# A three-stage transformer kernel whose per-sequence walk is written out in full instead of running as loops over two sequences

## The chip, the cores and the metric

The kernel runs on one core of one Trainium2 chip. The metric is the device time of one execution in microseconds (us), lower is better. Three runs of the kernel before gave 2319.28, 2320.09 and 2324.1 us, so the median is 2320.09 us.

## What is computed

There are 16 sequences of 512 tokens with 128 features, all float32. Two sandwiched blocks are applied to them:

```python
x = L0_attn_x                                     # (16, 512, 128)
x = x + layernorm(attn(layernorm(x)))             # 16 heads of 8, 4 key groups, causal, rotary
x = x + layernorm(ffn(layernorm(x)))
# ffn: two layers, each
#   qkv = shift_token(x) @ wqkv[l]                # 8 heads of 64
#   q, k = l2norm(q) * qs, l2norm(k) * ks; rotary with position scales
#   x = x + local_attention(q, k, v) @ wo[l]      # windows of 64, each looks one window back
#   h = layernorm(shift_token(x)) @ w1[l] + b1[l]
#   x = x + (a * gelu(g)) @ w2[l] + b2[l]
```

## The kernel before

The program has three stages, each in a block of its own with an instruction stream for every engine. `causal_attention` is the first main stage: it makes the first sandwich for the 16 sequences and leaves normalised, transposed activations in the SBUF buffer `u`. `local_layers` is the second main stage: two layers, each over the 16 sequences, `u` in and `u` out. `last_norm` is a short closing stage over four groups of four sequences.

In both main stages the order of the work is written out by hand as a list (`ORDER1`, `ORDER`). Each entry is a task with a part number. A *step* b runs the whole list once: part 0 tasks work on sequence b+1, part 1 tasks on sequence b, part 2 tasks on sequence b-1. So three sequences are in flight, and one sequence is finished in each step. In the first stage the last task of a step's part 2 is `copy_u` (line 532, ACT, two instructions); in the second it is `result` (line 1215, DVE, two instructions). The interval between two of these is the length of a step.

`walk` (lines 88 to 117) is called by each engine for itself and issues that engine's tasks. It writes step -1 (once) and steps 0, 1 and 2 straight out, then opens a hardware loop `eng.Fori(3, B - 2, 2)` whose body holds two steps, b and b+1; it runs six times, for steps 3 to 14, and so jumps back five times. Step 15 is again straight code. The second main stage does this once for each of its two layers. That makes 18 passes through a body and 15 jumps back in the whole program, on each engine: PE, ACT, DVE, POOL and SP (which issues the DMAs). The engines loop independently; there is no barrier at the end of a pass, only the semaphores of the tasks.

The order between engines is kept by semaphores that are only ever counted up. `Plan.linear` gives the value to wait for: where the sequence number is a Python integer it returns an integer; inside the loop the number is a register, and it returns `b * each + constant`, which the engine's sequencer works out with register instructions in front of the wait (seen in the profile at lines 140, 146, 151 and 286). The buffer slot (`slot`) is a Python integer in either case, since the body holds an even and an odd step. Line 113 is the loop itself: its register set-up, its compare and its branch.

Line 1272 holds the transposes of q and k on PE, line 1319 the products of probabilities and values.

Of the kernel before, what the change touches and what calls it, by code (L numbers as in the profile page):

```python
# [15 lines left out]
B, T, D = 16, 512, 128  # L16
# [71 lines left out]
def walk(eng, plan, tasks):  # L88

    def place(l, b, part):
        if not isinstance(b, int):
            return l, b + (1 - part)
        n = l * B + b + 1 - part
        return divmod(n, B) if 0 <= n < plan.depth * B else None

    def step(l, b, slot):
        for part, name, arg, *_ in plan.order:
            at = place(l, b, part)  # L100
            if at is None:
                continue
            for before, before_arg in plan.ahead(at[1], name, arg):
                if before in tasks:
                    tasks[before](*at, before_arg, slot ^ (part != 1))
            if name in tasks:
                tasks[name](*at, arg, slot ^ (part != 1))

    step(0, -1, 1)
    for l in range(plan.depth):  # L110
        for b in range(3):
            step(l, b, b % 2)
        with eng.Fori(3, B - 2, 2) as b:
            step(l, b, 1)
            step(l, b + 1, 0)
        step(l, B - 1, 1)
    step(plan.depth, 0, 0)


# [169 lines left out]
def causal_attention(nc, sem, ident, ident_bf, x1_v, u, x_v, Wq, bq, Wk, bk, Wv, bv, Wo, bo, cos1, sin1):  # L289
    with ExitStack() as ctx:  # L290
# [76 lines left out]
        def _(sp):  # L367
# [26 lines left out]
            for dst, src in loads:  # L394
                sp.dma_start(dst, src).then_inc(consts_loaded, 16)
            walk(sp, PLAN1, dict(load=load, load_again=load_again, store=store))
            for slot in range(2):
                sp.wait_ge(x1_stored[slot], 8 * B)

        @block.gpsimd  # L400
        def _(pool):
# [78 lines left out]
            def residual(l, b, arg, slot):  # L480
# [3 lines left out]
                pool.tensor_tensor(x1[:, slot], x_again[:, slot], z[:], ALU.add).then_inc(x1_made, 1)  # L484

            walk(pool, PLAN1, dict(apply=apply, rope_cos=rope_cos, rope_sin=rope_sin, rope_add=rope_add, copy_v=copy_v, low=low,
                                   select=select, residual=residual))

        @block.scalar
        def _(act):  # L490
# [38 lines left out]
            def copy_u(l, b, arg, slot):  # L529
                x, read = flow.to_read(act, "u_turn", 0, l, b)  # L530
                for r, first in ((slice(0, DH), 0), (slice(DH, P), 1)):
                    last = act.copy(u[r, bass.ds(b, 1), first:first + T].rearrange("p a t -> p (a t)"), x[r, :])
                last.then_inc(read, 1)

            walk(act, PLAN1, dict(seed=seed, copy_x=copy_x, copy_k=copy_k, copy_q=copy_q, copy_max=copy_max, exp=exp,
                                  copy_o=copy_o, copy_attn=copy_attn, copy_u=copy_u))

# [981 lines left out]
```

## Time and profile before

| | kernel before |
|---|---|
| median of three runs | 2320.09 us |
| the profiled execution, whole time | 2322.1 us |
| its span, first to last instruction | 2320.0 us |
| PE (matmuls) busy | 2048.2 us, 88% |
| DVE busy | 1819.0 us, 78% |
| ACT busy | 1634.9 us, 70% |
| POOL busy | 1381.1 us, 60% |
| mean granted TensorE clock | 0.948 |

PE is the tensor engine's matmuls and PEld its weight loads; they share one instruction stream. DVE, ACT and POOL are the vector, scalar and general engines. A *q* behind an engine's name (PEldq) means its sequencer: register instructions, branches and waits, which are not counted as busy time. [...] "issue" as the cause of an idle stretch means that the profile shows nothing that the engine waited for. Times in the rows are counted from the span's start.

### The profile page before, as it was taken

The page shows a single profiled execution, that of the slowest core. Times are in us where ns is not written, and L with a number is a line of the kernel's source. Part 1 is how long each engine was busy: PE and PEld are TensorE (multiplying, and loading weights), DVE is VectorE, ACT ScalarE, POOL GpSimd, SP SyncE. Part 2 cuts the span into 40 slices and gives each one's busy share as a digit, 9 for nine tenths or more (in the row PEclk, how much of TensorE's full clock was granted, in tenths as well). Part 3 has the DMA queues.
Part 4 walks back from the last instruction along what each step waited for, and adds up shares of the span by engine and source line. Part 5 has one row for each costly group of instructions (what it writes and reads, how often), then busy time and mean ns, then how long its engine had stood idle before and what let it go on. Part 6 is the DMA issues. An engine that isn't in the chain of part 4 may idle for free. (4 is left out here: it accounts for less than half of the span.)

```text
span 2320.0 us, 57840 instructions
## 1 busy us (share of the span) xinstructions
PE 2048.2 (88%) x20476; PEld 1354.5 (58%) x20476; DVE 1819.0 (78%) x3455; ACT 1634.9 (70%) x3312; POOL 1381.1 (60%) x2090
## 2 busy tenths in 40 slices
PE   2999999999999369999999999899999999999971
PEld 1555555555554256666666666566666666666641
DVE  2788788788786376988888888896898898798746
ACT  1676676676676266887787787786877787777745
POOL 3688787787786564655655655554564564564403
PEclk8999999999999579999999999999999999999985
DMA  1010000000000011010010010111011001001013
GB/s 35 2 28 16 16 24 19 16 18 26 15 15 20 28 48 32 18 34 18 18 34 18 18 34 18 28 34 31 18 25 28 19 20 32 18 18 34 18 37 110
DMA packets 50539, 60.13 MB, mean 26 GB/s; under 512 B 8144, under 2 KB 43392, under 8 KB 48256
## 3 DMA queue, kind: packets, MB, share of 16 engines
q1 hardware_dynamic: 50304, 56.58, 9.8%
q8 instruction: 199, 3.26, 0.6%
q14 instruction: 36, 0.29, 0.0%
HBM read 17.90 MB, written 8.39 MB: 11 GB/s over the span
## 5 line engine op out<-in xcount | busy, mean ns | idle before, releaser
L985 POOL TENSOR_TENSOR b_part_b<-b_raw,b_tabs 128x256 f32<-128x256 f32 x512 | 431.7, 874 | 345.6 <-ACT b_raw L1044 310.9
L994 POOL TENSOR_TENSOR b_qk<-b_qk,b_part_b 128x1024 f32<-128x1024 f32 x128 | 332.5, 2598 | 270.2 <-DVE b_qk L1144 263.0
L1144 DVE TENSOR_TENSOR b_qk<-b_raw,b_tabs 128x512 f32<-128x512 f32 x256 | 301.8, 1218 | 0.1
L1245 PE MATMUL b_work<-b_w_high,b_h_high 128*128 128x512 f32 x384 | 191.2, 498 | 31.0 <-DVE b_h_low L1134 19.2
L476 POOL TENSOR_SCALAR_AFFINE_SELECT a_probs<-a_probs 128x256 f32<-128x256 f32 x512 | 207.5, 418 | 0.0
L425 POOL TENSOR_TENSOR a_idle<-a_idle 128x1 f32<-128x1 f32 x432 | 84.7, 196 | 197.7 <-ACT a_probs L519 131.2
L1272 PE MATMUL b_work<-ident,b_qk 128*128 128x128 f32 x1024 | 162.1, 290 | 42.0 <-issue 32.0
L690 PE MATMUL a_work<-a_probs,a_v 128*32 128x512 f32 (+3 forms) x2048 | 182.2, 452 | 7.1 <-POOL a_probs L476 7.0
L1319 PEld LDWEIGHTS b_work<-b_v_even,b_pT 128*64 128x64 f32 x2048 | 140.8, 141 | 79.4 <-issue 76.7
L1272 PEld LDWEIGHTS b_work<-ident,b_qk 128*128 128x128 f32 x1024 | 127.1, 149 | 87.7 <-issue 65.1
L1065 ACT ACTIVATE b_probs<-b_sb,b_neg_max 128x128 f32<-128x128 f32 x512 | 147.9, 384 | 41.4 <-DVE b_neg_max L1166 41.0
L587 DVE TENSOR_REDUCE a_qpack<-a_pc 128x2 f32<-128x768 f32 (+1 forms) x128 | 139.4, 1089 | 43.9 <-PE a_pc L658 41.9
L1319 PE MATMUL b_work<-b_v_even,b_pT 128*64 128x66 f32 x2048 | 171.9, 231 | 2.0 <-ACT b_pT L1071 0.8
L1071 ACT COPY b_pT<-b_work 128x512 f32<-128x512 f32 x256 | 154.2, 602 | 25.4 <-PE b_work L1309 25.2
L1319 PE MATMUL b_work<-b_v,b_pT 128*64 128x66 f32 x2048 | 172.1, 232 | 0.0
L1033 ACT ACTIVATE b_sq<-b_work 128x1024 f32<-128x1024 f32 x128 | 131.5, 1027 | 56.6 <-PE b_work L1247 53.8
L1138 DVE TENSOR_REDUCE b_ss<-b_sq 128x16 f32<-128x1024 f32 x128 | 155.2, 1212 | 20.7 <-ACT b_sq L1033 17.5
L1160 DVE TENSOR_TENSOR b_qk<-b_qk,b_rs 128x1024 f32<-128x1024 f32 x128 | 163.9, 1282 | 4.9 <-POOL b_qk L994 2.2
L587 DVE TENSOR_REDUCE a_qpack<-a_pa 128x2 f32<-128x1024 f32 (+3 forms) x128 | 148.1, 1157 | 18.8 <-PE a_pa L658 14.4
L1309 PE MATMUL b_work<-ident,b_probs 128*128 128x128 f32 x1024 | 158.0, 278 | 4.6 <-ACT b_kT L1052 2.8
L1173 DVE RECIPROCAL b_rden<-b_work 128x4 f32<-128x4 f32 x256 | 45.5, 178 | 144.7 <-PE b_work L1319 140.0
L1309 PEld LDWEIGHTS b_work<-ident,b_probs 128*128 128x128 f32 x1024 | 126.0, 143 | 53.9 <-issue 36.3
(211 smaller groups left out, 5642.7 us busy)
## 6 DMA issues: line engine op xcount, KB each, us to landing
b_v_even<-b_v SPq DMA_DIRECT2D x32, 528.0 KB, 4.4
b_v_even<-b_v SPq DMA_DIRECT2D x32, 396.0 KB, 5.8
a_x_in<-in_L_attn_x SPq DMA_DIRECT2D x16, 256.0 KB, 3.5
a_x_again<-in_L_attn_x SPq DMA_DIRECT2D x16, 256.0 KB, 3.5
x_scratch<-a_x SPq DMA_DIRECT2D x16, 256.0 KB, 2.4
out<-c_y SPq DMA_DIRECT2D x4, 1024.0 KB, 5.4
b_w_raw<-in_L_ffn_wqkv SPq DMA_DIRECT2D x2, 768.0 KB, 4.3
b_tabs<-tab SPq DMA_DIRECT2D x2, 512.0 KB, 4.0
```

What stands on the lines that cost most here:

```text
L476: last = pool.affine_select(out=a, in_=a, compare_op=ALU.is_ge, fill=0.0, base=0, pattern=[[0, 2], [1, P]], channel_multiplier=-1)
L587: dve.tensor_reduce(qpack[:, slot, i, js[0]:js[-1] + 1, two, NEG_MAX].rearrange("p j g -> p g j"), x[:, :, 0:len(js) * w].rearrange("p g ( ...
L690: last = pe.matmul(bank_of[which][groups(g), s * P:T], v[:, slot, s, g, :], probs_of(j, fill + g % 2)[:, g // 2, col:col + T - s * P], sta ...
L985: last = pool.tensor_tensor(part_b[:, x, :].rearrange("p (h d) -> p h d", d=DH)[:, :, lo:lo + DH // 2], raw[:, i % 2, x, :].rearrange("p ( ...
L994: pool.tensor_tensor(qk[:, i], qk[:, i], part_b[:], ALU.add).then_inc(c_made, 1)
L1138: dve.tensor_reduce(ss[:, i * 16:(i + 1) * 16], sq[:].rearrange("p x (h d) -> p (x h) d", d=DH), AX, ALU.add).then_inc(ss_made, 1)
L1144: last = dve.tensor_tensor(qk[:, i, x, :].rearrange("p (h d) -> p h d", d=DH), raw[:, i % 2, x, :].rearrange("p (h d) -> p h d", d=DH), ta ...
L1160: dve.tensor_tensor(a, a, rs[:, i * 16:(i + 1) * 16].rearrange("p (h a) -> p h a", a=1).to_broadcast([P, 16, DH]), ALU.mult).then_inc(scal ...
L1245: pe.matmul(x, h_high[:, t], w_high[:, cols], start=True, stop=False)
L1272: last = pe.transpose(x[:, p * P:(p + 1) * P], qk[:, i, which, p * P:(p + 1) * P], ident[:])
L1309: last = pe.transpose(x[:, i * P:(i + 1) * P], probs[:, h % 4, i, :], ident[:])
L1319: last = pe.matmul(x[half_rows(w), i * VW:(i + 1) * VW], pT[:, h % 4, w * WIN:(w + 1) * WIN], values_, start=True, stop=True)
```

## The change

`walk` no longer opens the hardware loop. All 16 steps are a Python loop, so every step is straight code with a Python integer as its number, on all five engines, in the first stage and in both layers of the second. Task functions, their order, slots and buffers stay as they are. `last_norm` keeps its own loop, which makes one pass and never jumps back.

```diff
@@ -108,12 +108,8 @@
 
     step(0, -1, 1)
     for l in range(plan.depth):
-        for b in range(3):
+        for b in range(B):
             step(l, b, b % 2)
-        with eng.Fori(3, B - 2, 2) as b:
-            step(l, b, 1)
-            step(l, b + 1, 0)
-        step(l, B - 1, 1)
     step(plan.depth, 0, 0)
```

## Rows read from the trace of the kernel before

**Rows 1.** The page: span, and busy time of the engines.
```profile
span 2320.0 us, 57840 instructions
...
PE 2048.2 (88%) x20476; PEld 1354.5 (58%) x20476; DVE 1819.0 (78%) x3455; ACT 1634.9 (70%) x3312; POOL 1381.1 (60%) x2090
```

**Rows 2.** Timeline of ACT, first stage: start, length; ends of steps 1, 2, 4, 5, 14.
```profile
135.30 1.18 ACT L532 COPY u<-a_work 64x512 f32<-64x512 f32 x2
...
177.62 1.18 ACT L532 COPY u<-a_work 64x512 f32<-64x512 f32 x2 [0.15 <-PE a_work L619]
...
262.46 1.17 ACT L532 COPY u<-a_work 64x512 f32 x2 [0.40 <-PE a_work L619]
...
310.28 1.18 ACT L532 COPY u<-a_work 64x512 f32 x2 [0.42 <-PE a_work L619]
...
705.76 1.18 ACT L532 COPY u<-a_work 64x512 f32 x2 [0.41 <-PE a_work L619]
```

**Rows 3.** Timeline of DVE, first layer: ends of steps 1, 2, 4, 5, 14.
```profile
915.42 1.52 DVE L1215 SCALAR_TENSOR_TENSOR u<-b_work,b_bias,b_x 64x512 f32<-64x512 f32 x2 [0.30 <-PE b_work L1368]
...
957.10 1.51 DVE L1215 SCALAR_TENSOR_TENSOR u<-b_work,b_bias,b_x 64x512 f32<-64x512 f32 x2 [0.30 <-PE b_work L1368]
...
1040.69 1.51 DVE L1215 SCALAR_TENSOR_TENSOR u<-b_work,b_bias,b_x 64x512 f32 x2 [0.37 <-PE b_work L1368]
...
1085.32 1.52 DVE L1215 SCALAR_TENSOR_TENSOR u<-b_work,b_bias,b_x 64x512 f32 x2 [0.37 <-PE b_work L1368]
...
1478.58 1.52 DVE L1215 SCALAR_TENSOR_TENSOR u<-b_work,b_bias,b_x 64x512 f32 x2 [0.37 <-PE b_work L1368]
```

**Rows 4.** Timeline of DVE, second layer: ends of steps 1, 2, 14.
```profile
1622.02 1.52 DVE L1215 SCALAR_TENSOR_TENSOR u<-b_work,b_bias,b_x 64x512 f32<-64x512 f32 x2 [0.30 <-PE b_work L1368]
...
1663.70 1.51 DVE L1215 SCALAR_TENSOR_TENSOR u<-b_work,b_bias,b_x 64x512 f32<-64x512 f32 x2 [0.30 <-PE b_work L1368]
...
2187.89 1.51 DVE L1215 SCALAR_TENSOR_TENSOR u<-b_work,b_bias,b_x 64x512 f32 x2 [0.37 <-PE b_work L1368]
```

**Rows 5.** Instructions of the loop line 113, then register sums at 151: ns min/median/max.
```profile
L113 DVEq COMPARE_BRANCH  x18: 50/56/80, 260.7 to 2189.7; - x18
...
L113 PEldq COMPARE_BRANCH  x18: 83/3449/3891, 261.9 to 2188.8; - x18
...
L113 ACTq COMPARE_BRANCH  x18: 40/45/50, 262.6 to 2188.8; - x18
...
L151 PEldq ALU_OP  x1506: 32/32/36, 179.8 to 2186.7; - x189
```

**Rows 6.** Timeline: PE's first matmul behind two jumps back, idle time in brackets.
```profile
1045.10 0.65 PE L1272 MATMUL b_work<-ident,b_qk 128*128 128x128 f32 x4 [2.95 <-issue]
...
1132.00 1.05 PE L1272 MATMUL b_work<-ident,b_qk 128*128 128x128 f32 x4 [3.44 <-issue]
```

**Rows 7.** Busy time by window: steps 5 and 7 of the first stage, 7 and 2 of the second.
```profile
263.60:311.50 47.90, 44.12 (x434) 25.80 (x438) 36.14 (x79) 30.89 (x50) 34.92 (x86) 0.93 0.06 18
...
353.80:398.40 44.60, 41.41 (x434) 24.96 (x438) 36.08 (x79) 30.82 (x49) 34.84 (x85) 1.00 0.07 19
...
1128.60:1175.40 46.80, 42.37 (x423) 29.72 (x423) 37.39 (x63) 34.57 (x78) 24.61 (x23) 0.96 0.10 22
...
1623.50:1665.20 41.70, 40.83 (x422) 28.20 (x422) 37.45 (x63) 34.24 (x78) 24.61 (x23) 1.00 0.11 25
```
The columns are: window, its length, busy us (and instructions) of PE, PEld, DVE, ACT and POOL, granted clock, DMA share, GB/s.

**Rows 8.** Instruction DMA queues (packets, MB, share): whole page, then window 1623.5 to 1665.2.
```profile
q8 instruction: 199, 3.26, 0.6%
q14 instruction: 36, 0.29, 0.0%
...
q8 instruction: 4, 0.07, 0.6%
q14 instruction: 2, 0.02, 0.1%
```

**Rows 9.** The same, window 1052 to 1484, passes 2 to 6 of one loop; no other instruction queue.
```profile
q8 instruction: 42, 0.69, 0.7%
```

## The prediction

> **What bounds the kernel now.** I read the page first, then the length of each step, then the loop's own line, then the windows. The page shows PE as the busiest engine, 88% of the span, ahead of DVE at 78% [rows 1]. That says who sets the pace on average, not what the loop costs. For that the kernel holds its own comparison: some steps are already straight code and some run in the loop, with the same tasks. The timelines give their lengths as differences of starts. In the first stage straight step 2 takes 177.62 - 135.30 = 42.32 us; steps 3 and 4, in the loop with no jump back before them, take (262.46 - 177.62) / 2 = 42.42 us; step 5, the first behind a jump back, takes 310.28 - 262.46 = 47.82 us [rows 2]. In the first layer it is 41.68, 41.80 and 44.63 us [rows 3], and in the second layer straight step 2 takes 41.68 us [rows 4]. So a step has a settled pace of 42.3 or 41.7 us, the same in either form of code, and only steps behind a jump are long. I saw this in all 15 of them, every second step from 5 to 13 in each of the three loops (excess 2.3 to 5.5 us), and in no other step of the loops.
>
> In a settled step PE is busy 40.83 of 41.7 us, DVE 37.45, ACT 34.24 and POOL 24.61 [rows 7]. PE is the bound there, and a stall of PE is not won back: the step after a long one takes the settled time again.
>
> **What a jump back costs.** The instructions of line 113 name the engine. The compare-and-branch takes 0.056 us on DVE and 0.045 us on ACT in the median, but 3.449 us on PE, up to 3.891; PE's shortest, 0.083, is at the loop's exit, where it doesn't jump [rows 5]. [...] Behind two such jumps PE's matmuls stand idle for 2.95 and 3.44 us with "issue" as the only cause [rows 6], so what PE lacks there is instructions and not data. The instruction queues fit this. Queue 8 moves 16 KB packets (3.26 MB / 199) all through the span, in loops as well: 42 in 432 us [rows 8, 9]. Queue 14, 8 KB packets, moves 2 in a straight step and none in passes 2 to 6 of a loop [rows 8, 9]. I read queue 8 as PE's, which fetches its body anew in each pass and waits at the jump for the first block; and queue 14 as that of the other engines, which keep their short bodies.
>
> There is a second cost. Of the 15 long steps 11 show a granted clock below 1.00, such as 0.93 and 0.96 with 47.9 and 46.8 us; the other four stay at 1.00 and are shorter, such as 44.6 us [rows 7]. The half-speed stretch begins right behind the stall. In the first layer the idle time of 2.95 us at full clock made a step longer by 44.63 - 41.80 = 2.83 us [rows 3, 6]; the one of 3.44 us with the clock at 0.96 made it longer by 46.8 - 41.80 = 5.0 us [rows 3, 6, 7]. About 1.5 us of that is the clock.
>
> **The change part by part.**
> 1. *Jumps back, clock drops and register work of 36 steps.* I take all of it together, by replacing 12 steps of each loop by 12 straight ones of the same stage. First stage: 705.76 - 177.62 = 528.14 us against 12 x 42.32 = 507.84, which saves 20.3 us [rows 2]. First layer: 1478.58 - 957.10 = 521.48 against 12 x 41.68 = 500.16, which saves 21.3 us [rows 3]. Second layer: 2187.89 - 1663.70 = 524.19 against 500.16, which saves 24.0 us [rows 4]. The sum is 65.6 us. From below it comes out alike: 15 stalls at about 3 us are 45, 11 clock drops at 1.5 are 17, and the steps without a jump are 0.10 to 0.12 us shorter in straight code, which over 36 steps is 4; together 66 us.
> 2. *Register instructions.* They go on all engines; the largest group is 1506 on PE at 0.032 us, or 48 us of PE's sequencer [rows 5]. I give nothing more for them than the 0.1 us a step already counted, because PE's queued matmuls cover them: it is busy 40.83 us of a settled step [rows 7]. No wait is added, and no task changes place.
> 3. *New instruction fetches.* DVE, ACT, POOL and SP now stream their code in the 30 steps of passes 2 to 6 too, which they didn't. At about 1.5 blocks a step (2 in the window of rows 8) that is some 45 blocks of 8 KB. Lower bound: nothing, since the straight step with two such blocks is also the 41.68 us one, the shortest there is [rows 4, 8]. Upper bound: each is exposed like PE's jump, 45 x 3.45 = 155 us [rows 5]. I take nothing, by the row that shows the very thing. PE's own fetches get slightly fewer, since no pass starts over.
> 4. *Outside the 36 steps* (filling, the layer change, steps 15 and the last stage) the code is the same. TensorE's clock drops there too, and whether one falls in or out may shift with the phase; I allow three either way, 3 x 1.5 = 4.5 us.
>
> Sum: 2322.1 - 65.6 = 2256.5 us for the profiled execution. The median of the runs lies 2.0 us below that execution, so I predict 2254.5 us.
>
> [...]
>
> **The rivals.**
> - *A. The clock drops stay.* If TensorE's clock falls for a reason of its own about once in two steps, the 11 drops stay at 1.5 us: 2254.5 + 17 = 2271 us. Against it: all drops inside the loops stand behind a stall, and the straight or jump-free steps in the windows read 1.00 [rows 7]. A milder form, a few fetches of item 3 partly exposed, ends in the same region.
> - *B. The wait is not the jump's.* If PE lacks something at that point of the order that a straight program lacks as well, only the 0.10 to 0.12 us a step go: 2320.1 - 4 = 2316 us, no measurable change. Against it: steps 3 and 4 and all straight ones pass the same point without it [rows 2, 3].
> - *C. Slower, by exposed fetches of the other engines.* The place is item 3: an engine that reaches the end of its fetched code before the next block is there, while PE waits for its result. It decides from 65.6 / 45 = 1.5 us lost a block; at PE's 3.45 us it would be 2254.5 + 155 = 2410 us. For it: passes 2 to 6 show no such fetches, so most of the program has never run with them. Against it: the straight steps, and an engine that needs a new block only every two steps or so has 80 us to get it.
> - *D. Another engine takes over as the bound.* DVE at 37.45 of 41.7 us is nearest [rows 7]; it has 4 us of room a step, and straight steps show that it doesn't bind. It would cost at most what steps 3 and 4 show, 0.1 us a step, so 4 us; this lies inside the forecast's range.
>
> **How the numbers follow.** Forecast, with D: 0.84. A: 0.08. B: 0.04. C: 0.04. A measurement of this kernel can tell some 0.2%, 4.6 us, from no change; forecast and A are faster by more, B lies within, C is slower. The low end is the forecast less the clock drops of item 4, 2254.5 - 4.5 = 2250 us. The high end takes in A with a little of its milder form: 2272 us. B and C, 0.08, are left out, and about as much for the forecast's own tails.
>
> **What the changed profile would show.** Item 1: no compare-and-branch of line 113, intervals between the ends of steps of 42.3 us in the first stage and 41.7 us in the second for all steps from 2 to 14, and a granted clock of 1.00 in them. If A holds, the intervals are uneven by 1.5 us. If B holds, PE has idle stretches of 3 us with "issue" at the same matmuls of line 1272 [rows 6]. Item 2: fewer than 57,840 instructions [rows 1], no register sums. Item 3: queue 14 shows some 80 packets in place of 36 and queue 8 about 165 in place of 199; if C holds, DVE, ACT or POOL stand idle with "issue" for over a microsecond at such packets. The prediction is wrong if the settled pace itself differs from the straight steps' 42.32 and 41.68 us by more than 0.3 us.

## The result and the profile after

The changed kernel takes 2255.57 us in the median of four runs (2253.6 to 2257.88); the kernel before, run beside it, 2321.53 us (2319.28 to 2324.1). The ratio is 0.9716, 95% interval 0.9699 to 0.9733, so 2.8% faster (a ratio here and below is a kernel's time over that of the kernel before). The profiled execution took 2256.49 us with a span of 2254.8 us.

The page of the changed kernel first, the lines that answer to rows 1 and 8: span, busy times, and the two instruction queues (packets, MB, share).

```profile
span 2254.8 us, 52451 instructions
...
PE 2030.4 (90%) x20476; PEld 1343.0 (60%) x20476; DVE 1822.7 (81%) x3455; ACT 1633.3 (72%) x3312; POOL 1379.3 (61%) x2090
...
q8 instruction: 165, 2.70, 0.5%
q14 instruction: 78, 0.64, 0.1%
```

The engines do the same instructions as before (the counts behind the x are those of rows 1), 5,389 sequencer instructions are gone, and PE is busy 18 us less, about the 17 us that the prediction gives for the 11 clock drops in the loops, which are gone. Queue 8 moved 34 packets fewer and queue 14 moved 42 more.

The ends of steps, as in rows 2 to 4 (`copy_u` is now at line 528, `result` at 1211). First stage, ends of steps 1, 2, 4, 5 and 14:

```profile
136.30 1.18 ACT L528 COPY u<-a_work 64x512 f32<-64x512 f32 x2
...
178.60 1.18 ACT L528 COPY u<-a_work 64x512 f32<-64x512 f32 x2
...
263.18 1.18 ACT L528 COPY u<-a_work 64x512 f32<-64x512 f32 x2
...
305.47 1.18 ACT L528 COPY u<-a_work 64x512 f32<-64x512 f32 x2
...
686.03 1.18 ACT L528 COPY u<-a_work 64x512 f32<-64x512 f32 x2
```

Steps 2 and 5 take 42.30 and 42.29 us; step 5 took 47.82 us before [rows 2]. The 12 steps from 178.60 to 686.03 take 507.43 us, where they took 528.14. In the two layers, ends of steps 2 and 14 of each:

```profile
937.24 1.52 DVE L1211 SCALAR_TENSOR_TENSOR u<-b_work,b_bias,b_x 64x512 f32<-64x512 f32 x2 [0.30 <-PE b_work L1364]
...
1437.51 1.52 DVE L1211 SCALAR_TENSOR_TENSOR u<-b_work,b_bias,b_x 64x512 f32<-64x512 f32 x2 [0.30 <-PE b_work L1364]
...
1622.32 1.51 DVE L1211 SCALAR_TENSOR_TENSOR u<-b_work,b_bias,b_x 64x512 f32<-64x512 f32 x2 [0.30 <-PE b_work L1364]
...
2122.58 1.51 DVE L1211 SCALAR_TENSOR_TENSOR u<-b_work,b_bias,b_x 64x512 f32<-64x512 f32 x2 [0.30 <-PE b_work L1364]
```

That is 500.27 and 500.26 us for 12 steps each, 41.69 us a step, against 521.48 and 524.19 before [rows 3, 4]. The three differences are 20.7, 21.2 and 23.9 us, together 65.9 us; the span fell by 65.2 us, so the rest of the program is 0.6 us longer.

Busy time by window for steps 5 and 7 of the first stage and step 7 of the first layer, columns as in rows 7:

```profile
264.30:306.60 42.30, 40.99 (x430) 24.72 (x428) 36.41 (x79) 30.73 (x49) 34.67 (x86) 1.00 0.07 20
348.90:391.20 42.30, 41.00 (x430) 24.74 (x428) 36.42 (x80) 30.75 (x49) 34.67 (x86) 1.00 0.07 20
1105.50:1147.20 41.70, 40.84 (x423) 28.23 (x423) 37.45 (x63) 34.25 (x78) 24.60 (x23) 1.00 0.11 25
```

The granted clock (third number from the end, the share of TensorE's full speed) is 1.00 in all three, where two of them read 0.93 and 0.96 before [rows 7]. Before, it read 0.50 from 1132.2 to 1135.4 us, behind the jump at 1128.0, and 1.00 from 1126 to 1132. The busy times of DVE, ACT and POOL are unchanged within 0.4 us; only the time in which PE stood still, or ran slowly, is missing.

### The profile page after: what moved, and what is told of

Read it like the earlier page. It is cut to its first block and busy times, and to the rows that moved or that the text cites. A ratio compares the mean times of both kernels' runs of the same rounds, so it can differ in the third digit from the quotient of the medians.

```text
span 2254.8 us, 52451 instructions
## 1 busy us (share of the span) xinstructions
PE 2030.4 (90%) x20476; PEld 1343.0 (60%) x20476; DVE 1822.7 (81%) x3455; ACT 1633.3 (72%) x3312; POOL 1379.3 (61%) x2090
## 3 DMA queue, kind: packets, MB, share of 16 engines
q1 hardware_dynamic: 50304, 56.58, 10.1%
## 5 line engine op out<-in xcount | busy, mean ns | idle before, releaser
L1268 PE MATMUL b_work<-ident,b_qk 128*128 128x128 f32 x1024 | 157.2, 284 | 12.3 <-DVE b_qk L1156 9.9
L1242 PE MATMUL b_work<-b_w_low,b_h_high 128*128 128x512 f32 x384 | 153.9, 401 | 0.0
```

Of the source, the lines that this page charges most:

```text
L1268: last = pe.transpose(x[:, p * P:(p + 1) * P], qk[:, i, which, p * P:(p + 1) * P], ident[:])
```

## The experiments

The prediction came out, so the question is whether it did so for its reason. The theory: PE's jump back holds its sequencer for some 3.4 us because the instructions at the loop's head have to be fetched, and TensorE's clock falls behind many of these stalls (11 of 15). Rival 1: jumps and register work of all engines together. Rival 2: a taken jump on PE costs that much by itself. Rival 3: the new fetches harm in another way, for instance as data traffic. Each time below is a median of four runs or more, and the kernel before was run beside each, at 2321.0 to 2322.7 us.

The trace of the kernel before already says when PE's blocks come. While the first branch of the first layer waits (1041.58 us, 3.36 us long), queue 8 moves one packet; window 1041.6 to 1045:

```profile
q8 instruction: 1, 0.02, 1.8%
```

It is so at each of the 15 jumps back: one packet of queue 8 starts 0.94 to 1.56 us after the branch does, and none starts during the three branches at the loops' exits, which take 0.083 us.

### PE alone in straight code, and all others alone

```diff
+        if str(eng.engine).endswith("PE"):        # the other run: if not ...
+            for b in range(B):
+                step(l, b, b % 2)
+            continue
         for b in range(3):
             step(l, b, b % 2)
         with eng.Fori(3, B - 2, 2) as b:
```

> Only PE runs straight code; DVE, ACT, POOL and SP keep the loop over two sequences. My theory: the cost is PE's jump back (stall of some 3 us and the clock drop behind it, 15 times), so this has nearly the whole gain: 2256 to 2260 us, steps of 42.3 to 42.4 and 41.7 to 41.8 us, granted clock 1.00 in them. Rival 1, the cost lies in the jumps and register work of all engines together: a good part of the 66 us stays, 2275 us or more.

> The opposite half: DVE, ACT, POOL and SP run straight code, PE alone keeps the loop. My theory: the 15 stalls of PE and their clock drops stay, and only 0 to 0.1 us a step goes: 2316 to 2321 us, PE's compare-and-branch still 3.3 to 3.9 us. Rival 1 (all engines together): 2305 us or less. If the other engines' instruction fetches cost anything, it shows here as steps without a jump that are longer than 41.8 us.

With PE alone straight the time is 2256.17 us (2255.66 to 2259.53), ratio 0.9720 (0.9704 to 0.9736): the whole gain. With the other four straight and PE looping it is 2317.37 us (2315.26 to 2321.05), ratio 0.9985 (0.9975 to 0.9994): 4 us. Rival 1 falls. The instructions of the loop's line, first in the run with PE alone straight, then in the run with the others straight (ns min/median/max), and behind each the instruction queues of its page:

```profile
L117 DVEq COMPARE_BRANCH  x18: 50/56/80, 261.6 to 2126.5; - x18
...
L117 ACTq COMPARE_BRANCH  x18: 40/45/50, 263.3 to 2125.6; - x18
...
q8 instruction: 165, 2.70, 0.5%
q14 instruction: 36, 0.29, 0.0%
```

```profile
L117 PEldq COMPARE_BRANCH  x18: 82/3528/3852, 261.5 to 2184.4; - x18
...
q8 instruction: 199, 3.26, 0.6%
q14 instruction: 78, 0.64, 0.1%
```

Queue 8 changes with PE's code and queue 14 with that of the others, so the reading of the queues in the prediction is right. In the second run the steps of the layers that follow no jump fell from 41.80 to 41.69 us although the other engines now stream their code: the 42 added blocks of queue 14 cost nothing that shows. With PE alone straight they stay at 41.8 us. So in the layers the 0.1 us a step of the loop form belongs to the other engines; in the first stage these steps take 42.33 to 42.39 us with the others straight and hardly change. The 4 us are a rough figure (95% interval 1.4 to 5.8). Over the 36 steps of the traces, PE alone straight is only 2.2 us longer than the changed kernel, and the medians are 0.6 us apart.

### A longer body: four steps a pass

```diff
-        with eng.Fori(3, B - 2, 2) as b:
+        with eng.Fori(3, B - 4, 4) as b:
             step(l, b, 1)
             step(l, b + 1, 0)
+            step(l, b + 2, 1)
+            step(l, b + 3, 0)
```

> All engines loop, but over four steps: three passes and two jumps back in each of the three loops, 6 instead of 15. My theory, a cost for each jump of (2321.5 - 2255.6) / 15 = 4.4 us whatever the length of the body: nine of them go, 39 us, so about 2282 us (2279 to 2286). A body of twice the size might also cost the other engines their first block: then their compare-and-branch is over 1 us too, but it runs beside PE's, and the time stays within 3 us of that. Rival, the cost grows with the body that has to be fetched again: 6 x 8.8 = 53 us stay, 2309 us.

Measured: 2286.09 us (2282.18 to 2286.36), ratio 0.9845 (0.9828 to 0.9861). The six jumps left cost (2286.1 - 2255.6) / 6 = 5.1 us each, against 4.4 for the 15 of the kernel before. The cost goes with the number of jumps; the rival that it doubles with the body falls, but the jumps did get somewhat dearer. Two reasons lie with PE: its branch had one value of 4.99 us, above all of those before, and the step behind that one is the longest of the run (49.0 us); and the clock fell behind five of the six jumps, against 11 of 15. A third shows on the other engines. DVE's first instructions behind the jump that opens a pass, in this kernel:

```profile
1115.73 0.42 DVE L1176 TENSOR_TENSOR b_o_norm<-b_work,b_rden 128x256 f32<-128x256 f32 x1
1118.82 1.23 DVE L1162 TENSOR_TENSOR b_qk<-b_qk,b_rs 128x1024 f32<-128x1024 f32 x1 [2.66 <-issue]
```

At the same place of the run with two steps and a hint, below, the idle time is 0.24 us. So in the layers DVE, and ACT with 2.07 us in place of none, now wait behind the jump too, and their longer bodies are fetched anew (queue 14: 129 packets). Their compare-and-branch itself stays at 0.06 us and doesn't show it, though the expectation had looked for it there. The wait stands in the idle time behind the branch. Beside PE's own stall it adds little: where the clock fell, the layers' steps behind a jump take 46.4 to 46.8 us, as before (46.3 to 46.9). Only in step 11 of the second layer, 46.2 us with the clock at 1.00 where such steps took 44.6 to 45.0 before, may it have shown; that is one step of one trace.

### The same loop with a prefetch hint for PE's jump

In this run PE has one instruction more at the head of each pass, `BRANCH_PREFETCH_HINT` in the trace (18 of them, 0.031 us in the median).

```diff
-        with eng.Fori(3, B - 2, 2) as b:
+        with eng.bass.Fori(3, B - 2, 2, engines=[eng.engine],
+                           hint_back_edge=str(eng.engine).endswith("PE")) as b:
```

> All engines loop over two steps as before, but PE's jump carries a prefetch hint for its target, given at the head of each pass. If PE's 3.4 us is the wait for the block of instructions at the loop's head, the compare-and-branch falls to about 0.1 us, the clock drops go, and only the 0.1 us a step of the loop form stays: 2257 to 2262 us, with small code. If the jump costs for another reason (emptying of the queue, decoding), nothing changes: 2318 to 2323 us.

Measured: 2262.19 us (2260.7 to 2264.8), ratio 0.9747 (0.9731 to 0.9763). The loop is whole; only the hint is new. The loop's line on PE and the queues:

```profile
L113 PEldq COMPARE_BRANCH  x18: 80/216/261, 261.1 to 2128.6; - x18
...
q8 instruction: 64, 1.05, 0.2%
q14 instruction: 36, 0.29, 0.0%
```

The jump takes 0.216 us instead of 3.449 [rows 5], the steps in the loops take 42.2 to 42.4 us in the first stage and 41.8 to 41.9 us in the layers (step 3 of the second layer 42.1), and the clock drops in them are gone. Queue 8 moves no packet at all from a loop's first branch to its last, where it moved 8 or 9 a pass before. So the fetch isn't merely made earlier: with the hint PE runs passes 2 to 6 from what it holds. Together with the fetch the wait has gone; before, each of the 15 waits had a fetch inside it. This shows the cause: the wait was the fetch of the target. Why PE fetches its body anew without the hint is not shown. What stays over the run with PE straight, 6.0 us between the medians and 3.5 between the profiled spans, is mostly one place: step 15 of the first stage, behind the loop's exit, takes 43.72 us instead of 39.09.

### Short jumps

The changed kernel with 36 tiny loops of two passes on PE, one ahead of each of the steps 3 to 14:

```diff
         for b in range(B):
+            if 3 <= b < B - 1 and str(eng.engine).endswith("PE"):
+                with eng.Fori(0, 2, 1):
+                    eng.sem_inc(SHORT_JUMPS[0], 1)
             step(l, b, b % 2)
```

> The changed kernel with one thing added on PE: ahead of each of the steps 3 to 14 of the three straight parts stands a tiny loop of two passes (its body raises an unused semaphore by one), so PE takes 36 jumps back to a target a few instructions behind. If the cost of a jump is the fetch of a far target, these jumps take 0.1 to 0.3 us each, are mostly hidden by the matmuls in PE's queue, and the time is 2256 to 2266 us, granted clock 1.00 in the steps. If a taken jump on PE costs 3.4 us by itself, 36 x 3 us and clock drops come on top: over 2360 us.

Measured: 2260.02 us (2259.37 to 2260.73), 4.4 us over the changed kernel, 0.12 us a place. In the trace the 36 branches taken last 0.207 to 0.231 us and the 36 not taken 0.076 us:

```profile
L116 PEldq COMPARE_BRANCH  x72: 76/142/231, 178.0 to 2084.7; - x72
```

Rival 2 falls: a jump to a near target takes 0.207 to 0.231 us on PE, the far one 3.449 [rows 5].

### PE's sequencer held without a far jump

In place of a jump back, the same tiny loop with 7 passes stands ahead of steps 5, 7, 9, 11 and 13 of each straight part; in a second run, 4 passes.

```diff
         for b in range(B):
+            if b in (5, 7, 9, 11, 13) and str(eng.engine).endswith("PE"):
+                with eng.Fori(0, 7, 1):           # the other run: 4
+                    eng.sem_inc(HOLDS[0], 1)
             step(l, b, b % 2)
```

> The changed kernel, and at the 15 places where the kernel before jumped back (ahead of steps 5, 7, 9, 11 and 13 of each straight part) PE's sequencer is held by a tiny loop of 7 passes, at 0.52 us a pass after the run with short jumps: about 3.4 us, without any far jump or new fetch. My theory, that the loss is only the sequencer's standstill and the clock drop which follows: the time returns to that of the kernel before less the 0.1 us a step of its loop form, 2313 to 2322 us, and half-speed stretches return behind the holds. Rival, that the far jump harms in another way too (data traffic of the new fetches, the other engines' loops): clearly less, 2300 us or under.

> As the run with holds, with 4 passes instead of 7: about 1.8 us a hold. In the kernel before, a jump of 3.36 us made the step 2.8 us longer, so PE's queue hid some 0.6 us. If the clock doesn't drop behind so short a hold, 15 x 1.2 = 18 us come on top of 2255.6: 2274 us. If it drops as often as behind the long ones, 11 x 1.5 more: 2290 us. This tells the part of the clock from that of the standstill.

Measured: 2310.87 us (2308.89 to 2313.34) with 7 passes, just under the range I gave, and 2270.67 us (2270.3 to 2274.21) with 4. The first long step of the first layer (5) and the next one (7) of the run with 7 passes, by window, then step 5 of the run with 4 passes, each with PE's first matmul behind the hold:

```profile
1037.20:1083.30 46.10, 42.31 (x423) 29.67 (x423) 37.49 (x62) 34.50 (x78) 24.58 (x23) 0.96 0.09 22
1125.00:1169.70 44.70, 40.75 (x423) 28.24 (x423) 37.48 (x63) 34.14 (x78) 24.61 (x23) 1.00 0.10 23
...
1040.12 0.65 PE L1275 MATMUL b_work<-ident,b_qk 128*128 128x128 f32 x4 [3.00 <-issue]
```

```profile
1026.70:1069.70 43.00, 40.72 (x423) 28.20 (x423) 37.51 (x63) 34.14 (x78) 24.60 (x23) 1.00 0.10 23
...
1028.12 0.65 PE L1275 MATMUL b_work<-ident,b_qk 128*128 128x128 f32 x4 [1.47 <-issue]
```

A hold of some 3.6 us by harmless instructions brings the picture of the kernel before back: the same matmuls of line 1272 (here 1275) stand idle 3.00 us (2.95 before [rows 6]), steps are 44.7 us at full clock and 46.1 us where it fell (44.63 and 46.8 before [rows 3, 7]), and the clock fell behind 9 of the 15 holds (11 of 15 before). That accounts for 2310.87 - 2255.57 = 55.3 us. Of the 10.1 us that are missing to the kernel before, some 4.0 (1.4 to 5.8) are the loop form of the other engines and 3.1 are two drops fewer at 1.55 us. Most of the other 3.0 us is in the length of the stalls: PE's idle stretches behind the 15 jumps sum to 43.3 us, those behind the 15 holds to 40.5. Nothing clear of noise is left for rival 3. With the shorter hold PE is idle 1.47 us at this place and the step 1.3 us longer, and no clock drop occurs behind any of the 15: 15.1 us in all. In the first stage the stalls are shorter in every run, 2.0 us behind the long holds and 0.4 to 0.5 behind the short ones, and the steps are 2.3 and 0.7 us longer. This tells the two parts apart. At full clock a stall costs about its idle time; the drop adds 1.5 us in the first stage (46.1 against 44.6 us) and 1.6 in the layers (46.14 against 44.54 on average) where it occurs.

### Four steps with hints: can the loop be made as good?

> All engines loop over four steps (two jumps back in each loop) and PE's jump carries the hint. PE's body is now some 3,700 instructions. With two steps a pass and the hint, queue 8 fetched only 64 packets, so PE ran the passes from what it held. If the hint works only where the whole body is held, PE's compare-and-branch is 3.5 us again: 2283 to 2287 us. If the hint fetches the target block ahead, it is 0.2 us and queue 8 shows over 150 packets. What is left then is the wait of DVE and ACT, 2.4 to 3.5 us behind each of the six jumps in the run with four steps, no longer hidden beside PE's: 2260 us if their slack in a step takes it up, 2262 + 6 x 3 = 2280 us if all of it is exposed.

> Loops over four steps with the hint on every engine. In the run with the hint on PE alone, DVE and ACT waited 2.4 to 3.1 us behind each of the six jumps, and the steps there were 45.6 us instead of 41.8. If this wait of theirs is the whole of what stayed, it goes with their hints: 2260 to 2266 us, no step of the loops over 42.5 us. If PE's own late blocks (its branch took up to 2.8 us with the hint) set those steps, little changes: 2278 to 2284 us.

Both have the four-step body of above. With the hint on PE alone: 2283.54 us (2280.38 to 2286.93). With hints on all engines: 2281.24 us (2279.67 to 2285.09). The loop's line on PE in each of the two, first PE alone, and the queues of the first:

```profile
L113 PEldq COMPARE_BRANCH  x9: 87/375/2793, 347.9 to 2149.0; - x9
...
q8 instruction: 182, 2.98, 0.5%
q14 instruction: 128, 1.05, 0.2%
```

```profile
L113 PEldq COMPARE_BRANCH  x9: 87/375/3510, 346.0 to 2150.3; - x9
```

In the first, the jumps of the first layer take 0.36 and 0.38 us on PE with queue 8 at 182 packets, none of them from 14.6 us before each of these two branches until 1.1 to 1.2 us behind its start. So with the hint the loop's head was there at the jump, though PE fetched anew in every pass. Whether it was fetched ahead or kept is not shown. Yet the steps behind them take 45.7 and 45.6 us, with the clock at 0.96. DVE still waits 2.7 and 2.5 us there, ACT 2.2 and 2.4. With their own hints these two steps fall to 42.5 and 42.2 us at clock 1.00, and queue 14 moves no packet in these passes, so the other engines' waits are real costs once PE's no longer covers them. Neither case of the first run's expectation held alone: PE's branch took 0.4 us in the first layer, but 1.3 to 2.8 in the other two loops. But my expectation of 2260 to 2266 us for that run missed. In the first stage PE's branch took 3.5 and 3.4 us in spite of its hint (1.35 and 2.79 with the hint on PE alone), and in the second layer 1.7 and 1.5 us. The two medians are 2.3 us apart, less than either run's spread, so which engines carry hints made no difference that can be told. The other part is the exit. Behind the exit of the first layer's loop PE waits although it doesn't jump (run with all hints):

```profile
1459.32 0.29 PEld L1312 LDWEIGHTS b_work<-ident,b_probs 128*128 128x128 f32 x2 [4.96 <-issue]
```

and that step 15 takes 55.8 us instead of 49.6. Queue 8 moved no packet from 1438.88 us until 1457.04, 4 us behind the branch of the exit, so there too PE lacked a block of instructions; in the kernel before the last packet ahead of this exit came 3.5 us before the branch. That the hint is what holds the next block up is inferred from the runs side by side: step 15 is 0.9 to 6.2 us longer than in the changed kernel at five of the nine exits of the three runs with hints, and at none of the nine exits of the unhinted runs in which PE loops. Why the hint takes PE's wait away at some jumps of a long body and not at others stays open; no run here tells it.

## Why the prediction was right

- **Forecast and range.** 2254.5 us, measured 2255.57. The range of 2250 to 2272 held it. The sum for the profiled execution, 2256.5 us, was met at 2256.49; four runs lie between 2253.6 and 2257.88, so that the last microsecond agrees is luck.
- **Which cost it is.** The step rested on PE's 3.449 us at line 113 and on the idle matmuls. The runs with PE alone straight (2256.17 us), with the hint (branch 0.216 us) and with short jumps (0.21 us) show that it is PE, and that it is the far target's fetch; the runs with holds bring the loss back without one.
- **Item 1, 65.6 us,** measured 65.9 over the same 36 steps. Comparing steps of one form with steps of the other inside one trace gave the size without any model of fetches. The three loops came out at 20.7, 21.2 and 23.9 us, where 20.3, 21.3 and 24.0 had been read. The count from below held in kind as well. The stalls were put at 15 x 3 = 45 us, and PE's idle stretches behind the 15 jumps sum to 43.3 (2.0 to 2.5 us each in the first stage, 3.0 to 3.5 in the layers). The drop of the clock was put at 1.5 us and the holds show 1.5 to 1.6. The work of the loop form was put at 4 us; the run with the other engines straight shows 4.0, but with an interval of 1.4 to 5.8, and the steps behind no jump of the traces show about 2.
- **Item 2.** Register work hidden beside PE: right for PE. The 0.1 us a step that does show comes from the other engines, since with PE alone straight the layers' steps stay at 41.8 us; the prediction had left open on which engine it arises.
- **Item 3,** nothing for the new fetches: right. It forecast some 80 and 165 packets; there are 78 and 165.
- **Item 4,** up to 4.5 us from the rest: it came to 0.6 us.
- **Rival A** (clock drops stay) is refuted by steps at 1.00, and by the holds, which bring drops back where the stall is long. **Rival B** fell with the hint run. **Rival C** (the other engines' fetches exposed) is wrong for straight code. Its mechanism is real in another place: with four steps a pass DVE and ACT wait 2 to 3 us behind their jumps in the layers. **Rival D** (another engine takes over) did not come: steps take 41.69 us with DVE busy for 37.45.

## What to carry to other kernels

Where a loop's body is long, compare a step behind the jump with one that isn't, and look at the compare-and-branch of the busiest engine and the idle time behind it. In this kernel the steps behind the 15 jumps, with the 0.1 us a step of the loop form, held 65.6 us, and straight code gave 65.9. Here only the engine that sets the pace had to be written out: PE alone gave all 65 us. A prefetch hint on its jump gave 59 us with the code still a loop, but with four steps a pass it did not take the cost away (2283.54 us with it on PE, 2286.09 without), and it cost something at the exit (step 15 of the first stage, 43.72 us instead of 39.07).

## What the runs showed of the hardware that I had not expected

- PE can hold a whole body of two steps. With the hint it fetched 64 packets of 16 KB in all and none in passes 2 to 6; without it it fetched the body again in every pass (199 packets in all), although it would fit.
- On PE the wait for the target stands in the branch's own duration (3.4 us); on DVE and ACT the branch reads 0.05 us and the wait stands behind it as "issue" (2.66 and 2.07 us in the layers, with four steps a pass). A look at branch durations alone misses it.
- With a hint on a jump that is then not taken PE can lose time behind the exit: 4.96 us idle in one place, and a step of 43.72 instead of 39.07 us in another. Five of nine exits show it.
- The clock fell behind 9 of 15 equal holds (3 of 5 with PE idle for 2.0 us in the first stage, 6 of 10 with 2.9 to 3.2 us in the layers) and behind none of the 15 shorter ones (0.4 to 0.5 and 1.3 to 1.6 us idle).
